# Bias dot products with one operand in PSUM, and the first twelve LoRA matmuls in another order

## The reference

```python
# layer 0: a mixture of masked expert weights
masked_w = weight * mask[None, :, :]
w_bot = jnp.einsum('bg,got->bot', y, masked_w)
x = x + jnp.einsum('bnt,bot->bno', x, w_bot) + bias
# layer 1: a base weight and a LoRA term of rank 16 per expert, SCALING = 2
out = jnp.einsum('btc,oc->bto', x, W_base) + b_base
h = jnp.einsum('btc,erc->bter', x, As)
lora = jnp.einsum('bter,eor,be->bto', h, Bs, w)
x = x + out + lora * SCALING
```

## Time and profile before

| | us |
|---|---|
| median of 3 runs | 57.27 |
| lowest and highest | 57.02 and 57.6 |
| the profiled execution | 57.23 |
| its span, first to last instruction | 55.4 |
| PE busy in it | 51.7 |
| DVE busy in it | 42.1 |
| ACT busy in it | 31.5 |
| POOL busy in it | 31.2 |

### The profile page before, as it was taken

How to read it: one execution, slowest core, us unless ns; L and a number is a source line. 1 busy time by engine, 2 the same in 40 slices (tenths; PEclk the granted TensorE clock), 3 DMA queues, 4 the chain that set the end, 5 groups by cost and what they waited for, 6 DMA issues and landing times.

```text
span 55.4 us, 997 instructions
## 1 busy us (share of the span) xinstructions
PE 51.7 (93%) x342; PEld 47.1 (85%) x342; DVE 42.1 (76%) x64; ACT 31.5 (57%) x52; POOL 31.2 (56%) x30
## 2 busy tenths in 40 slices
PE   2999999999999999999999999999999999999900
PEld 2988999999999888988998898899889889888800
DVE  0039999979596998999999999979929959805030
ACT  1949900447807889440999925970993950840800
POOL 4003400299980099999909999999966990000000
PEclk9999999999999999999999999999999999999999
DMA  0699999999999994000082540090054045049572
GB/s 0 133 392 335 373 366 389 419 418 425 408 396 417 417 393 169 9 0 0 0 306 78 222 169 0 15 364 0 6 195 183 0 185 194 0 179 382 197 284 95
DMA packets 5476, 11.79 MB, mean 213 GB/s; under 512 B 608, under 2 KB 1376, under 8 KB 5472
## 3 DMA queue, kind: packets, MB, share of 16 engines
q1 hardware_dynamic: 5184, 11.35, 54.6%
q10 hardware_dynamic: 288, 0.39, 1.9%
HBM read 7.54 MB, written 4.19 MB: 212 GB/s over the span
## 4 chain that ended last, share of the span: by engine, by line
PE 93%; DVE 1%; issue 0%
PE ps_out L441 13%; PE ps_out L483 13%; PE ps_out L445 13%; PE ps_out L449 13%; PE ps_merge L441 7%; PE ps_merge L445 7%; PE ps_merge L449 7%; PE ps_merge L522 6%; PE ps_lora L441 5%; PE ps_lora L445 5%; PE ps_lora L449 5%; DVE out_sb L432 1%; PE ps_lora L547 1%; DVE warm L310 0%
## 5 line engine op out<-in xcount | busy, mean ns | idle before, releaser
L189 POOL TENSOR_TENSOR W_lo<-W,W_hi 128x512 fp32r<-128x512 f32 x8 | 10.5, 1314 | 7.1 <-ACT W_hi L235 7.1
L342 DVE TENSOR_TENSOR x_lo<-x_sb,x_hi 128x1024 fp32r<-128x1024 f32 x8 | 12.7, 1584 | 0.0
L195 POOL TENSOR_TENSOR W_lo<-W,W_hi 128x512 fp32r<-128x512 f32 x6 | 10.9, 1824 | 0.0
L441 PE MATMUL ps_out<-x_hi,M_hi 128*128 128x512 f32 (+1 forms) x32 | 9.8, 388 | 0.0
L445 PE MATMUL ps_out<-x_lo,M_hi 128*128 128x512 f32 (+1 forms) x32 | 9.7, 384 | 0.0
L449 PE MATMUL ps_out<-x_hi,M_lo 128*128 128x512 f32 (+1 forms) x32 | 9.7, 384 | 0.0
L248 ACT ACTIVATE M_hi<-ps_merge 128x512 fp32r<-128x512 f32 x8 | 4.8, 597 | 8.0 <-PE ps_merge L449 8.0
L255 ACT ACTIVATE x_hi<-x_sb 128x1024 fp32r<-128x1024 f32 x8 | 8.4, 1053 | 0.0
L199 POOL TENSOR_TENSOR W<-W,ident 128x256 f32<-128x256 f32 x6 | 6.6, 1099 | 3.0 <-DVE x_lo L342 3.0
L357 DVE TENSOR_SCALAR out_sb<-ps_out,bias_sb 128x512 f32<-128x512 f32 x7 | 5.2, 747 | 3.5 <-PE ps_out L449 3.4
L264 ACT ACTIVATE out_sb<-ps_out,bias_sb 128x512 f32<-128x512 f32 x8 | 5.5, 685 | 3.9 <-PE ps_out L449 2.2
(11 more groups left out here) (50 smaller groups left out, 80.1 us busy)
## 6 DMA issues: line engine op xcount, KB each, us to landing
x_sb<-xT_dram SPq DMA_DIRECT2D x8, 512.0 KB, 10.2
outT_dram<-out_sb SPq DMA_DIRECT2D x15, 256.0 KB, 2.3
packs_sb<-packs_dram SPq DMA_DIRECT2D x7, 288.0 KB, 5.3
rows_sb<-rows_dram SPq DMA_DIRECT2D x1, 384.0 KB, 6.8
base_sb<-base_dram ACTq DMA_DIRECT2D x1, 256.0 KB, 3.6
outT_dram<-out_sb SPq DMA_DIRECT2D x2, 128.0 KB, 1.8
packs_sb<-head_dram SPq DMA_DIRECT2D x1, 192.0 KB, 3.4
packs_sb<-rest_dram SPq DMA_DIRECT2D x1, 160.0 KB, 3.6
```

Of the source, the lines that this page charges most:

```text
L189: pool.tensor_tensor(W1_lo[:, b % W1BUF], W1[:, b % W1BUF], W1_hi[:, b % W1BUF].bitcast(f32), ALU.subtract).then_inc(w1lo_done, 1)
L195: pool.tensor_tensor(W0_lo[:, b % 2], W0[:, b], W0_hi[:, b % 2].bitcast(f32), ALU.subtract).then_inc(w0lo_done, 1)
L342: nc.vector.tensor_tensor(x_lo[:, b % XBUF], x_sb[:, b], x_hi[:, b % XBUF].bitcast(f32), ALU.subtract).then_inc(xlo_done, 1)
L441: nc.tensor.matmul(out, hi_l, hi_r, start=(n == 0), stop=False)
```

## The change

In `dot`, the second operand is `ps_row` in place of `bias0_row`. `ps_row` is the second half of `ps_lora[1]`. ACT fills it with one copy of 128 x 256 after `split_x_hi(0)`, once the rows have landed and DVE's `w1(3)` has read that PSUM tile. DVE waits for this copy before the first dot product, and waits for the bias matmuls (`bias_mm`) ahead of the other two dot products, where it did so after them.

On PE, `lora(0)` and `lora(1)` are replaced by `lora_first()`: the same twelve matmuls, with the first hi·hi matmul of sample 1 moved in behind the second matmul of sample 0. The later `lora(b)` wait for `alo_done` ahead of their first matmul and no longer wait for it in the middle.

```diff
+        ps_row = ps_lora[1][:, 1, :]
...
             w1_hi(2)
             split_x_hi(0)
+
+            act.wait_ge(rows_in, 16)
+            act.wait_ge(w1_done, 4)
+            nc.scalar.activation(ps_row, bias0_row, ACT.Copy).then_inc(row_done, 1)
             for b in range(2):
                 act.wait_ge(eye_second, 1)
...
             def dot(row, out):
 
-                return nc.vector.tensor_tensor_reduce(out=row_products[:, :], in0=row, in1=bias0_row, scale=1.0,
+                return nc.vector.tensor_tensor_reduce(out=row_products[:, :], in0=row, in1=ps_row, scale=1.0,
                                                       scalar=0.0, op0=ALU.mult, op1=ALU.add, accum_out=out)
...
+            dve.wait_ge(row_done, 1)
             dve.wait_ge(rows_in, 16)
             dot(A_er, A_bias0[:, :]).then_inc(dots_done, 1)
...
+            dve.wait_ge(bias_mm, 1)
             for j in range(NT):
                 dve.wait_ge(dots_done, 1 + j)
                 dot(base_rows[:, j, :], base_bias0[:, j:j + 1]).then_inc(dots_done, 1)
             dve.wait_ge(dots_done, 1 + NT)
-
-            dve.wait_ge(bias_mm, 1)
             for j in range(NT):
...
+            def lora_first():
+
+                def term(b, j, left, right, first=False, last=False):
+                    return nc.tensor.matmul(ps_lora[b][:, j, :], left[:, b, j * P:(j + 1) * P], right[:, :],
+                                            start=first, stop=last)
+
+                pe.wait_ge(bhi_done, 1)
+                pe.wait_ge(ahi_done, 1)
+                term(0, 0, A_hi, B_hi, first=True)
+                pe.wait_ge(blo_done, 1)
+                term(0, 0, A_hi, B_lo)
+                pe.wait_ge(ahi_done, 2)
+                term(1, 0, A_hi, B_hi, first=True)
+                pe.wait_ge(alo_done, 1)
+                term(0, 0, A_lo, B_hi, last=True)
+                term(0, 1, A_hi, B_hi, first=True)
+                term(0, 1, A_hi, B_lo)
+                term(0, 1, A_lo, B_hi, last=True).then_inc(lora_mm, 1)
+                term(1, 0, A_hi, B_lo)
+                pe.wait_ge(alo_done, 2)
+                term(1, 0, A_lo, B_hi, last=True)
+                term(1, 1, A_hi, B_hi, first=True)
+                term(1, 1, A_hi, B_lo)
+                term(1, 1, A_lo, B_hi, last=True).then_inc(lora_mm, 1)
+
             def lora(b):
 
-                pe.wait_ge(ahi_done, b + 1)
-                if b == 0:
-                    pe.wait_ge(bhi_done, 1)
-                if b >= 2:
-                    pe.wait_ge(w1_done, b - 1)
+                pe.wait_ge(alo_done, b + 1)
+                pe.wait_ge(w1_done, b - 1)
                 if b == 5:
                     pe.wait_ge(bias_done, 1)
...
-                                 [(A_hi[:, b, cols], A_lo[:, b, cols], B_hi[:, :], B_lo[:, :])],
-                                 lo_ready=(alo_done, b + 1),
-                                 mid_ready=(blo_done, 1) if b == 0 and j == 0 else None)
+                                 [(A_hi[:, b, cols], A_lo[:, b, cols], B_hi[:, :], B_lo[:, :])])
...
-            lora(0)
-            lora(1)
+            lora_first()
```

More of the change, by code:

```diff
@@ L121, in conditional_residual_kernel @@
         base_done, dots_done, low_done, fixed_done = sem("base_done"), sem("dots_done"), sem("low_done"), sem("fixed_done")
-        bias_mm, bias_done, bhi_done, blo_done = sem("bias_mm"), sem("bias_done"), sem("bhi_done"), sem("blo_done")
+        row_done, bias_mm, bias_done, bhi_done, blo_done = sem("row_done"), sem("bias_mm"), sem("bias_done"), sem("bhi_done"), sem("blo_done")
         ahi_done, alo_done = sem("ahi_done"), sem("alo_done")
```

## The result

| | before | after |
|---|---|---|
| median, executions run side by side | 57.24 us (6) | 58.52 us (6) |
| lowest and highest of these | 57.02 and 58.25 | 58.07 and 58.73 |
| ratio, 95% interval | | 1.0207, 1.0163 to 1.025 |
| the profiled execution | 57.23 | 58.6 |
| its span | 55.4 | 56.8 |

The changed kernel is 2.1% slower, where no change was forecast. Executions of either kernel lie mostly near 57.3 us or near 58.5 us, with some between; those of 57.9 us or more I call late, and since the ratios leave out what lies over 1.5% above a kernel's own fastest, the count of late executions stands beside them. Of the ten executions of the changed kernel (these six and four later ones, g4) nine are late.

What follows compares the result with a forecast made beforehand. The prediction took PE's queue to bound the kernel. It summed -0.08 us for the first matmuls and 0 each for copy, dot products and moved waits, from 57.27 to 57.2 us, range 56.8 to 57.5.

Steps and rivals of the forecast that it cites:

- What bounds the kernel: Whole kernel: PE's queue sets the end, PE being busy 51.7 of 55.4 us and 93% of the last chain.
- The first matmuls: PE's first twelve matmuls: the new order saves 0.18 us, 0.10 after the rate rise, 0.08 past `lora(2)`.
- rival B: PE's rate rises at another time: earlier gives 57.27, after the twelve matmuls 57.09; chance 0.25, of it 0.15 early.
- the main case: Whole kernel: the summed terms hold, 0.08 us saved on PE, median 57.2 us; chance 0.55.
- ACT's copy: ACT's copy into PSUM starts at about 15.95, takes 0.36 to 0.6 us inside idle time, and costs 0.
- The dot products: On DVE ahead of the bias: 0.43 us each with the PSUM operand, so the bias is ready 1.5 us earlier.
- What the 1.5 us is worth at the end: End of the kernel: the earlier bias gains nothing; `out0(0)` and its store go earlier, PE found the bias ready anyway.
- C: Old dot products delay PE by 0.34 us in executions not profiled; the change removes that, 56.85 us; chance 0.10.
- E: ACT's copy overruns its idle time and PE loses 0.3 us, giving 57.5 us; chance 0.04.
- D: DVE's collisions with POOL move onto POOL's W_lo, PE stands 0.16 us, giving 57.35 us; chance 0.06.

Runs made afterwards that it cites:

- g4: The changed kernel run again with no further edit, for the spread of its executions and a second profile; median 58.65 us, 3 of 4 late.
- e1: Kernel before plus only the new order of the first twelve matmuls and the moved waits, dot products still from SBUF; 57.38 us, ratio 0.9988.
- f3: The changed kernel with 24 warm-up matmuls in place of 28; median 58.66 us, 4 of 4 late.
- h2: The changed kernel with one more DVE wait ahead of the bias, for the first half of sample 1's product; 57.28 us, ratio 0.9997.

## Why the prediction was wrong, point by point

**What bounds the kernel.** Right for the kernel before up to PE's last matmul. It stopped there: "So PE's queue sets the end" left the 2.73 us behind PE's last matmul out of the sum, and no row was read for the seven last stores.

**The first matmuls.** The mechanism was right, the rate rose elsewhere. In the profile after (PE's timeline):

```profile
4.52 0.50 PE L461 MATMUL ps_lora<-B_lo,A_hi 128*128 128x256 f32 x1
4.85 0.28 PE L461 MATMUL ps_lora<-B_hi,A_hi 128*128 128x256 f32 x1
4.97 0.32 PE L461 MATMUL ps_lora<-B_hi,A_lo 128*128 128x256 f32 x1
5.12 0.28 PE L461 MATMUL ps_lora<-B_hi,A_hi 128*128 128x256 f32 x1
...
10.13 0.19 PEld L447 LDWEIGHTS ps_lora<-B_hi,A_hi 128*128 128x128 f32 x1 [0.19 <-issue]
```

The spacing is 0.12 (2.4 GHz) from 4.85 on, so it is rival B's early case: PE got to `lora(2)` early and its weight load stood for 0.19 us. The view names no releaser, but `w1(0)` ends at 9.34 + 0.68 = 10.02 as before. PE then loaded at 10.13, the first time that the prediction gave for it, from the 0.11 of hand-over. The 0.08 went on as forecast, down to 14.54 in place of 14.62 for DVE's `w0(6)`, and to 0.11 at the last matmul. So the gain over the profiled execution of before was the 0.08 of the main case, though by B's way; over an execution of before with as early a rise it would be nothing, as B says. The order alone (e1) had the rise where it was before:

```profile
4.87 0.42 PE L458 MATMUL ps_lora<-B_hi,A_hi 128*128 128x256 f32 x1
5.09 0.42 PE L458 MATMUL ps_lora<-B_hi,A_lo 128*128 128x256 f32 x1
```

Four matmuls are through at 5.09 + 0.42 = 5.51, forecast 5.49. The twelfth starts 0.05 earlier than before, forecast 0.10. And there the packs, which "have landed before PE asks for them", came late once and cost 0.32 us, so that `lora(2)` began at 10.57. Less than 0.1 us is below what such a place varies by. In before, e1 and after the first of the twelve matmuls starts at 4.12 to 4.17 us in each, and the rise is at about 6.2, 6.2 and 4.8 us. This agrees with the Trainium skill (TensorE: Matmul & The Clock Gate, Part 1), by which the monitor's window runs freely and isn't tied to the kernel's start. The rise at 9.2 in f3 follows 0.43 us of idle time and can't be told apart from what that did.

**ACT's copy.** Right: at 15.93 for 0.39 us (forecast about 15.95, 0.36 to 0.6), hidden, with 0.60 us of idle time left behind it.

**The dot products.** Right: 0.41, 0.41 and 0.42, forecast 0.43, and alike. From the start of the pair to the bias it is 0.92 us where it was 2.44, so 1.52 less, forecast 1.5; the pair also starts 0.18 earlier, and so the bias comes 25.82 - 24.12 = 1.7 us earlier. This also agrees with the Trainium skill (SBUF — State Buffer, Who interferes with whom): a DVE instruction with at most one SBUF input, outside the modes that use two ports, doesn't contend with GpSimd.

**What the 1.5 us is worth at the end.** This is the step that failed. It said "out of the profile, nothing", and "`out0(0)` and its store go earlier" as if that had no price. For PE that holds: between 4.8 and 52.6 us it is busy for 47.7 of 47.8. But the kernel lost 1.3 us: with the dot products from PSUM, and DVE and ACT early, most executions were late (31 of 38, against 12 of 94 before), and every late one that was profiled, f3 apart, has a load of instructions among the last stores. The sum had no term for the tail. Put right it would be 57.2 with a chance of the tail's 1.5 us on top. Out of the trace of before alone the chance could not be had, but that there is a price could: a load on q8 comes at 56.49, 1.6 us behind the last store's landing (54.94), and q14's load at 28.09 had made one of 16 landings of two stores 0.7 and 0.8 us late, where nobody waited for them.

**The rivals.** C and E didn't show: h2, with all of the change and a bias no longer early, is even with before and not 0.4 us below it, and the copy didn't overrun. D, the collisions with POOL, was the one on the slower side, and sought the price of an early DVE on PE. The collision came (`split_x_lo(2)` at 25.90 took 1.57 us in place of 1.22), but POOL's W_lo, at 25.09 now, took 1.30 and PE had no hole. So that the change came out slower, as D has it, is luck and not D's mechanism: the time was lost at the stores. The range ended at 57.5 since all its cases were PE's. The Trainium skill (Runtime: NRT & Kernel Launch, Instruction fetch mechanics) says that engines' instructions are fetched in blocks of 16 KiB on a DMA queue of the sequencer's own, and calls the cost mostly hidden. The size agrees with q8's rows (q14's loads are of 8 KB); "mostly hidden" doesn't hold in this tail, where one block goes with 1.5 us.

## What to carry to other kernels

The end of the span isn't the end of the bounding engine: cost the stretch behind the last matmul as its own term, with the stores in it, each of which is through only with the last of its 16 landings, and look at what else (loads of instructions too) moves at that time. Making an engine off the critical path faster moves events in time, and what isn't on PE's path can still reach the end, through a buffer that a store holds or through the last store itself. When executions fall into two groups, count them: one profile of each kernel would have shown a cause here, but not how often it strikes.

## What the runs showed of the hardware

- A 16 KB load of instructions (q8) took 0.88 to 1.84 us of DMA engine time. Among the last stores it came with one of 16 landings 1.2 to 2.5 us late in the ten late profiles, and the changed kernel, late in 9 of 10 executions, was 1.3 us, or 2%, slower.
- In 20 traces with 340 stores, one landing was 0.3 us or more behind the other fifteen in 53 stores, each with a load of instructions under way, and in none of the 231 stores without one.
- The same program had its loads at 15.90, 30.47, 49.43 us in one execution and at 19.02, 30.46, 54.19 in another.
- In the profile with 24 warm-up matmuls (f3) PE had 0.43 us without matmuls ahead of the first product, its rate rose at about 9.2 us in place of 4.8 (after) or 6.2 (before), and its end was 1.43 us later than after.
- An ACT copy of 128 x 256 from SBUF to PSUM took 0.39 us; one within SBUF takes 0.36.
- A dot product of 128 x 256 with one operand in PSUM took 0.41 us beside POOL's work, where two SBUF operands took 0.66 to 1.39.
